# Attention scores leave their PSUM bank at the row maximum, and the exponential runs in place in SBUF

## The chip, the cores and the metric

One core of one Trainium2 chip runs the whole program in one launch. The metric is device time in microseconds (us). A core has TensorE (PE), VectorE (DVE), ScalarE (ACT) and GpSimd (POOL), a queue that issues the DMAs (SP), SBUF (128 partitions), and eight PSUM banks of 128 x 512 fp32 values.

## What is computed

A decoder layer over x of shape (4, 512, 512) fp32: self-attention with 16 heads of 32 columns, a mixing step with the weights of a context, and a feed-forward part of 4096 columns with packed 4-bit weights. The change touches the self-attention alone. Masked scores there are multiplied by zero, not set to minus infinity:

```python
scores = jnp.einsum('bthd,bshd->bhts', q, k)
mask = jnp.tril(jnp.ones((T, T), dtype=scores.dtype))
scores = scores * mask
attn = jax.nn.softmax(scores / T ** 0.5, axis=-1)
out = jnp.einsum('bhts,bshd->bthd', attn, v).reshape(B, T, H * Dh)
return out @ Wo
```

## The kernel before

The order on each engine is written out by hand; engines meet through semaphores. There are four batches n. The attention of a batch is a body of 16 units u (`UNITS`) between two stretches of other work (`between`: projections, the context, the mixing). Unit u takes the four heads of head group `u // 4` and the 128 query rows of tile `i = u % 4`; only the `wide[i]` = 128 (i + 1) keys at or below the diagonal are handled, the others through one exponential of the negated maximum (`exp_zero`, `masked_values`). In this text (u, j) is head j of unit u, and four units of one head group are called a group: units 8 to 11 are one.

For each (u, j) the steps are:

- `scores` (PE, L929): one matmul into `bank[j]`. Bank j is used by head j of every unit, so the matmul of (u + 1, j) waits until (u, j) has left it. Before, that is `exp_done` of (u, j).
- `row_max` (DVE, L1600): multiplies the scores by mask and factor and takes the row maximum. It writes the product back into `bank[j]`, and a second short instruction writes the maximum into `mx`.
- `shift` (POOL, L763): negates the maximum into `nmx`.
- `exp` (ACT, L1257): reads `bank[j]`, adds `nmx`, writes `prob[:, u % 2, j]` in SBUF; a second short instruction on the same line reads the sum into `den`.
- `turn` (PE, L940): transposes `prob` in blocks of 128 x 128 into bank 4, 5 or 7, which three turns, reciprocals and packed weights share in rotation; a turn waits for the reader of the one three places before it (`turn_read`).
- `turned` (ACT L1273, for three heads, or two in the last unit of a group; DVE L1610 for the others): copies the bank into `prob_t`.
- `values` (PE, L961): probabilities times values of a whole unit into bank 6; `recips` (PE, L970) and `recip_out` (ACT, L1279) lay out the reciprocals, `divide` (DVE, L1638) makes `o_sum`; `out_head` (ACT, L1285) and POOL's `out_tail` (L779) split a finished group.

PE's order sets much of the rest. In unit u it is

```python
for j in range(4):
    if u + 1 < UNITS:
        scores(n, u + 1, j)
    turn(n, u, j)
    ...
    if j == 3 and u > 0:
        recips(n, u - 1)
        if u < UNITS - 1:
            values(n, u - 1)
```

POOL converts packed weights (L756) beside it, PE and ACT repack them at j = 1 and j = 3 of the first unit of a group (`repack`, ACT's copy `pk_t` L1293). DVE's order in unit u is `row_max(u, 0)`, `divide`, `row_max(u, 1)`, then `all_tokens(u - 1)`, which waits for all four exponentials of unit u - 1, `row_max(u, 2)`, `row_max(u, 3)`, and a copy.

`prob` has other tenants between the bodies: the context's exponentials (`e_p`, half 1), the first block of weights and the operands of sums (half 0), which DMAs store from it.

Of the kernel before, what the change touches and what calls it, by code (L numbers as in the profile page):

```python
# [47 lines left out]
B, T, D = 4, 512, 512  # L48
# [43 lines left out]
def decoder_layer(nc, x, ctx_1024, Wq, Wk, Wv, Wo, xWq, xbq, xWk, xbk, gate_p, gate_s, up_p, up_s, down_p, down_s, out):  # L92
    with ExitStack() as ctx:
# [236 lines left out]
        def alone(eng, sem, value):  # L330

            eng.wait_ge(sem, value)
            eng.sem_inc(passed, 1)
# [539 lines left out]
        def _(pe):  # L873
# [43 lines left out]
            def scores(n, u, j):  # L917
                hg, i = u // TT, u % TT
                if i == 0 and j == 0:
                    for g in (2 * hg, 2 * hg + 1):  # L920
                        pe.wait_ge(stacked[g % 4], n * 128 + 64 * (g // 4) + 64)
                if u > 0:
                    pe.wait_ge(exp_done, n * ROWS + 4 * (u - 1) + j + 1)
                elif j == 2:
                    pe.wait_ge(v_out, n * TT + 3)
                elif j == 3:
                    pe.wait_ge(vb_out, n * (TT - 1) + TT - 1)
                h = 4 * hg + j
                pe.matmul(bank[j][:, 0:wide[i]], stack[:, 0, h, P * i:P * i + P], stack[:, 1, h, 0:wide[i]],  # L929
                          start=True, stop=True).then_inc(s_full, 1)  # L930
# [299 lines left out]
        def _(act):  # L1230
# [21 lines left out]
            def exp(n, u, j):  # L1252
                i = u % TT
                act.wait_ge(shift_done, n * ROWS + 4 * u + j + 1)
                if u >= 2:
                    act.wait_ge(t_full, n * ROWS + 4 * (u - 2) + j + 1)
                nc.scalar.activation(prob[:, u % 2, j, 0:wide[i]], bank[j][:, 0:wide[i]], ACT.Exp,  # L1257
                                     bias=nmx[:, u % 2, j:j + 1], accum_out=den[:, u % 2, j:j + 1]).then_inc(exp_done, 1)

            def exp_zero(n, u):  # L1260
# [131 lines left out]
            def between(n, prev, nxt):  # L1392
# [49 lines left out]
                    spread_heads(2, n, 4)  # L1442
                if nxt:
                    context_heads(n + 1, (0, 1))
                    if n == B - 2:
                        act.wait_ge(sums_stored, 16 * 8)
                    elif n >= 0:
                        act.wait_ge(first_stored, 16 * (3, 7)[n])
                    exp(n + 1, 0, 0)
                    exp(n + 1, 0, 1)  # L1450
                    context_heads(n + 1, (2, 3))
                    exp(n + 1, 0, 2)
                    exp(n + 1, 0, 3)
                    qkv_heads(n + 1, (11,))
# [28 lines left out]
            def body(n, last):  # L1483
                for u in range(UNITS):
                    for j in range(4):
                        if u == 1 and j == 0:
                            act.wait_ge(att_full, n * KT + KT)
                        if u > 0:
                            exp(n, u, j)
                        if j == 3 and u % TT < TT - 1:  # L1490
                            exp_zero(n, u)
                        if j == AT_OUT and u % TT == 2 and u > TT:
                            out_head(n, u // TT - 1)

                        if j >= 2:
                            turned(n, u, j - 2)
                        elif j == 0 and u > 0:
                            if copied_by_act(u - 1) > 2:
                                turned(n, u - 1, 2)
                        if j == 3 and u % TT == 0 and u > 0:  # L1500
                            repacked(n, u // TT - 1)
                        h = 4 * u + j - AT_RECIP
                        if h >= 0 and h % 4 == 0:
                            recip_out(n, h // 4)
                turned(n, UNITS - 1, 2)
                if not last:
                    spread_heads(0, n + 1, 0)
                for u in range((ROWS - 1 - AT_RECIP) // 4 + 1, UNITS - 1):
                    recip_out(n, u)
                repacked(n, HG - 1)  # L1510
                recip_out(n, UNITS - 1)
                out_head(n, HG - 1)
                between(n, True, not last)
# [28 lines left out]
        def _(dve):  # L1542
# [51 lines left out]
            def row_max(n, u, j):  # L1594
                i = u % TT
                if u >= 2:
                    dve.wait_ge(shift_done, n * ROWS + 4 * (u - 2) + j + 1)
                alone(dve, s_full, n * ROWS + 4 * u + j + 1)

                nc.vector.tensor_tensor_reduce(out=bank[j][:, 0:wide[i]], in0=bank[j][:, 0:wide[i]],  # L1600
                                               in1=mask[:, P * (3 - i):P * (3 - i) + wide[i]], scale=C_EXP,
                                               scalar=0.0 if i < TT - 1 else NEG, op0=ALU.mult, op1=ALU.max,
                                               accum_out=mx[:, u % 2, j:j + 1]).then_inc(max_done, 1)
# [215 lines left out]
            def between(n, prev, nxt):  # L1819
# [32 lines left out]
                    spread_tails(2, n, 4)  # L1852
                if nxt:
                    value_sum_out(n + 1, 2)
                    row_max(n + 1, 0, 0)
                    row_max(n + 1, 0, 1)
                    context_tails(n + 1, (0, 1))
# [177 lines left out]
```

## Time and profile before

| | us |
|---|---|
| median of 3 runs | 1482.5 (1481.33 to 1483.2) |
| profiled execution | 1482.48 |
| its span, first to last instruction | 1480.8 |
| PE busy in the span | 1426.6 (96%) |
| DVE busy | 990.7 (67%) |
| ACT busy | 716.4 (48%) |
| POOL busy | 380.2 (26%) |

The shares are means over very different stretches. The attention bodies lie at about 66 to 128, 196 to 260, 328 to 392 and 465 to 530 us of the span; behind the last comes the feed-forward part, with PE busy throughout. Times in the rows below are microseconds from the span's start.

### The profile page before, as it was taken

The page shows a single profiled execution, that of the slowest core. Times are in us where ns is not written, and L with a number is a line of the kernel's source. Part 1 is how long each engine was busy: PE and PEld are TensorE (multiplying, and loading weights), DVE is VectorE, ACT ScalarE, POOL GpSimd, SP SyncE. Part 2 cuts the span into 40 slices and gives each one's busy share as a digit, 9 for nine tenths or more (in the row PEclk, how much of TensorE's full clock was granted, in tenths as well). Part 3 has the DMA queues.
Part 4 walks back from the last instruction along what each step waited for, and adds up shares of the span by engine and source line. Part 5 has one row for each costly group of instructions (what it writes and reads, how often), then busy time and mean ns, then how long its engine had stood idle before and what let it go on. Part 6 is the DMA issues. An engine that isn't in the chain of part 4 may idle for free.

```text
span 1480.8 us, 26838 instructions
## 1 busy us (share of the span) xinstructions
PE 1426.6 (96%) x8896; PEld 720.5 (49%) x8896; DVE 990.7 (67%) x2125; ACT 716.4 (48%) x1660; POOL 380.2 (26%) x691
## 2 busy tenths in 40 slices
PE   6989998998998899999999999999999999999999
PEld 4465456556644654344444444444444444444444
DVE  7786688678668767887566666655765765665533
ACT  5795279239615945254353353353343442533432
POOL 0053225304363436512211112112112212212100
PEclk9999999999999999999999999999999999999999
DMA  7554522352454521000000001001001001000011
GB/s 249 136 166 125 155 86 81 111 163 66 147 154 137 195 81 45 17 16 33 22 13 32 17 17 33 17 17 35 17 17 32 17 16 33 17 17 1 0 58 57
DMA packets 76877, 98.01 MB, mean 66 GB/s; under 512 B 8000, under 2 KB 60736, under 8 KB 76224
## 3 DMA queue, kind: packets, MB, share of 16 engines
q1 hardware_dynamic: 76736, 96.23, 21.2%
q8 instruction: 76, 1.25, 0.4%
q14 instruction: 65, 0.53, 0.1%
HBM read 68.94 MB, written 27.26 MB: 65 GB/s over the span
## 4 chain that ended last, share of the span: by engine, by line
PE 83%; DVE 5%; issue 5%; ACT 4%; POOL 1%; DMA 1%; ACTq 0%; POOLq 0%; SPq 0%; DVEq 0%
PE bank L876 24%; PE bank L877 24%; PE bank L878 24%; PE bank L940 2%; ACT prob L1257 2%; PE bank L961 2%; PE bank L1016 1%; PE bank L929 1%; PE bank L889 1%; PE bank L970 1%; PE bank L1011 1%; PE bank L1001 1%; DVE xt L1585 1%; DMA pk_in<-L_ffn_down_W_packed_dram 1%; ACT prob_t L1273 1%
## 5 line engine op out<-in xcount | busy, mean ns | idle before, releaser
L876 PE MATMUL bank<-xs,G 128*128 128x512 f16 x896 | 339.8, 379 | 2.0 <-DVE c L1730 0.9
L878 PE MATMUL bank<-xs,G 128*128 128x512 f16 x896 | 339.6, 379 | 0.0
L877 PE MATMUL bank<-xs,G 128*128 128x512 f16 x896 | 339.6, 379 | 0.0
L1345 ACT COPY c<-bank 128x512 f32<-128x512 f32 x192 | 111.2, 579 | 220.0 <-PE bank L878 215.2
L1730 DVE TENSOR_TENSOR c<-bank,c 128x512 f32<-128x512 f32 x128 | 88.1, 689 | 193.0 <-PE bank L878 193.0
L876 PE MATMUL bank<-Wd,hid 128*128 128x512 f16 x512 | 194.1, 379 | 2.8 <-DVE X L1784 2.8
L878 PE MATMUL bank<-Wd,hid 128*128 128x512 f16 x512 | 194.0, 379 | 0.0
L877 PE MATMUL bank<-Wd,hid 128*128 128x512 f16 x512 | 194.0, 379 | 0.0
L748 POOL TENSOR_TENSOR c<-c,m 128x512 f32<-128x512 f32 x64 | 82.4, 1287 | 388.5 <-ACT c L1345 388.5
L1784 DVE SCALAR_TENSOR_TENSOR X<-bank,col,X 128x512 f32<-128x512 f32 x128 | 95.4, 750 | 101.5 <-PE bank L878 101.4
L1600 DVE CUSTOM_DVE_ANT_0 bank<-bank,mask,col 128x128 f32<-128x128 f32 (+3 forms) x256 | 139.1, 548 | 23.0 <-issue 17.8
L1257 ACT ACTIVATE prob<-bank,nmx 128x128 f32<-128x128 f32 (+3 forms) x256 | 145.7, 577 | 1.5 <-POOL nmx L763 0.9
L876 PEld LDWEIGHTS bank<-xs,G 128*128 128x128 f16 x896 | 87.6, 98 | 113.3 <-ACT c L1345 6.1
L878 PEld LDWEIGHTS bank<-xs,G 128*128 128x128 f16 x896 | 87.7, 98 | 105.8
L877 PEld LDWEIGHTS bank<-xs,G 128*128 128x128 f16 x896 | 87.7, 98 | 103.1
L940 PE MATMUL bank<-ident,prob 128*128 128x128 f32 x640 | 111.9, 277 | 13.3 <-ACT prob L1257 4.5
L1368 ACT CAST hid<-c 128x512 f16<-128x512 f32 x128 | 79.2, 619 | 90.3 <-DVE c L1744 87.2
L1360 ACT ACTIVATE c<-c,col 128x512 f32<-128x512 f32 x96 | 69.4, 723 | 94.1 <-DVE c L1730 94.1
L763 POOL TENSOR_TENSOR nmx<-zero,mx 128x1 f32<-128x1 f32 x256 | 51.1, 199 | 238.8 <-DVE mx L1600 215.5
L1750 DVE TENSOR_TENSOR hid<-c,hid 128x512 f16<-128x512 f32 x128 | 86.1, 712 | 25.7 <-ACT hid L1368 25.7
L705 POOL TENSOR_TENSOR w_sum<-w_full 128x384 f32<-128x384 f32 (+1 forms) x30 | 22.1, 738 | 314.2 <-DVE w_full L1711 314.1
L940 PEld LDWEIGHTS bank<-ident,prob 128*128 128x128 f32 x640 | 76.1, 140 | 31.3 <-issue 18.9
(192 smaller groups left out, 2409.1 us busy)
## 6 DMA issues: line engine op xcount, KB each, us to landing
stack<-qk_dram SPq DMA_DIRECT2D x128, 128.0 KB, 3.3
sc_in<-scale_t SPq DMA_DIRECT2D x30, 384.0 KB
qk_dram<-qk SPq DMA_DIRECT2D x32, 256.0 KB, 2.9
packed_t<-pk_t SPq DMA_DIRECT2D x32, 192.0 KB, 1.9
pk_in<-packed_t SPq DMA_DIRECT2D x30, 192.0 KB
X<-in_x_dram SPq DMA_DIRECT2D x4, 1024.0 KB, 5.7
pk_in<-L_ffn_gate_W_packed_dram SPq DMA_DIRECT2D x16, 256.0 KB, 2.7
pk_in<-n_L_ffn_up_W_packed_dram SPq DMA_DIRECT2D x16, 256.0 KB, 3.0
```

The costliest lines, as they stand in the source:

```text
L748: nc.gpsimd.tensor_tensor(c22[x][:], c22[x][:], m5[x][:], ALU.add).then_inc(c22_out, 1)
L876: pe.matmul(o, lhs(0), rhs(0), start=first, stop=False, skip_group_check=onto)
L877: pe.matmul(o, lhs(0), rhs(1), start=False, stop=False, skip_group_check=onto)
L878: return pe.matmul(o, lhs(1), rhs(0), start=False, stop=stop, skip_group_check=onto)
L940: mm = pe.transpose(turn_bank(slot)[:, P * k:P * k + P], prob[:, u % 2, j, P * k:P * k + P], ident[:])
L1257: nc.scalar.activation(prob[:, u % 2, j, 0:wide[i]], bank[j][:, 0:wide[i]], ACT.Exp, bias=nmx[:, u % 2, j:j + 1], accum_out=den[:, u % 2, ...
L1345: nc.scalar.copy(dst[:], bank[BANK_Y if which == M5 else x][:]).then_inc(c_copied, 1)
L1368: nc.scalar.copy(hid[:, beta, q, r, 0, :], quarter(1, idx)[:]).then_inc(hid_hi, 1)
L1600: nc.vector.tensor_tensor_reduce(out=bank[j][:, 0:wide[i]], in0=bank[j][:, 0:wide[i]], in1=mask[:, P * (3 - i):P * (3 - i) + wide[i]], sca ...
L1730: nc.vector.tensor_tensor(dst[:], bank[at][:], dst[:], ALU.add).then_inc(comb, 1)
L1750: nc.vector.tensor_tensor(hid[:, beta, q, r, 1, :], quarter(1, idx)[:], hid[:, beta, q, r, 0, :], ALU.subtract).then_inc(hid_lo, 1)
L1784: nc.vector.scalar_tensor_tensor(xv, bank[4 + t][:], C_OUT, xv, ALU.mult, ALU.add).then_inc(acc_out, 1)
```

## The change

The product of `row_max` goes to `prob` in SBUF instead of back into the bank. The exponential reads it there and writes over it. A bank is free as soon as the maximum is taken, so `scores` of (u + 1, j) waits for `max_done` of (u, j). The waits that protect `prob` move with its first writer, from ACT to DVE: the turn of two units before (`t_full`), the context's transposes (`att_full`), and the stores of what lay in half 0 (`first_stored`, `sums_stored`).

```diff
--- before.py
+++ after.py
@@ scores (PE)
                 if u > 0:
-                    pe.wait_ge(exp_done, n * ROWS + 4 * (u - 1) + j + 1)
+                    pe.wait_ge(max_done, n * ROWS + 4 * (u - 1) + j + 1)
@@ exp (ACT)
                 act.wait_ge(shift_done, n * ROWS + 4 * u + j + 1)
-                if u >= 2:
-                    act.wait_ge(t_full, n * ROWS + 4 * (u - 2) + j + 1)
-                nc.scalar.activation(prob[:, u % 2, j, 0:wide[i]], bank[j][:, 0:wide[i]], ACT.Exp,
+                nc.scalar.activation(prob[:, u % 2, j, 0:wide[i]], prob[:, u % 2, j, 0:wide[i]], ACT.Exp,
@@ between (ACT)
                     context_heads(n + 1, (0, 1))
-                    if n == B - 2:
-                        act.wait_ge(sums_stored, 16 * 8)
-                    elif n >= 0:
-                        act.wait_ge(first_stored, 16 * (3, 7)[n])
                     exp(n + 1, 0, 0)
@@ body (ACT)
-                        if u == 1 and j == 0:
-                            act.wait_ge(att_full, n * KT + KT)
@@ row_max (DVE)
                 if u >= 2:
                     dve.wait_ge(shift_done, n * ROWS + 4 * (u - 2) + j + 1)
+                    dve.wait_ge(t_full, n * ROWS + 4 * (u - 2) + j + 1)
+                elif u == 1 and j == 0:
+                    dve.wait_ge(att_full, n * KT + KT)
                 alone(dve, s_full, n * ROWS + 4 * u + j + 1)
 
-                nc.vector.tensor_tensor_reduce(out=bank[j][:, 0:wide[i]], in0=bank[j][:, 0:wide[i]],
+                nc.vector.tensor_tensor_reduce(out=prob[:, u % 2, j, 0:wide[i]], in0=bank[j][:, 0:wide[i]],
@@ between (DVE)
                     value_sum_out(n + 1, 2)
+                    if n == B - 2:
+                        dve.wait_ge(sums_stored, 16 * 8)
+                    elif n >= 0:
+                        dve.wait_ge(first_stored, 16 * (3, 7)[n])
                     row_max(n + 1, 0, 0)
```

No instruction is added, taken away or moved to another place on its engine. What differs is what they wait for and where they read and write. On PE, in unit 2 of a batch with the scores of unit 3 (L929) between the turns (L940), before:

```order
L929 MATMUL bank<-stack 128x512 [waits exp_done]
L940 MATMUL bank<-ident,prob 128x128 [waits rden_out,exp_done]
L940 MATMUL bank<-ident,prob 128x128 x2
L929 MATMUL bank<-stack 128x512 [waits exp_done]
L940 MATMUL bank<-ident,prob 128x128 [waits pt_act,exp_done]
```

and now:

```order
L929 MATMUL bank<-stack 128x512 [waits max_done]
L940 MATMUL bank<-ident,prob 128x128 [waits rden_out,exp_done]
L940 MATMUL bank<-ident,prob 128x128 x2
L929 MATMUL bank<-stack 128x512 [waits max_done]
L940 MATMUL bank<-ident,prob 128x128 [waits pt_act,exp_done]
```

The scores matmul keeps its place ahead of the turn, but no longer waits for the exponential that the turn behind it waits for. On DVE, the row maxima of unit 3 (128x512) with the small work between them, before:

```order
L1600 ISA bank,mx<-bank,mask,col 128x512 [waits shift_done,s_full]
L1600 ISA mx 128x1
L1618 SCALAR_TENSOR_TENSOR den_all<-e_zero,den 128x4 [waits e_zero_done,exp_done]
L1600 ISA bank,mx<-bank,mask,col 128x512 [waits shift_done,s_full]
L1600 ISA mx 128x1
L1628 RECIPROCAL r_col<-den_all 128x4 [waits den_done]
```

and now (the lines after the edits are five lower):

```order
L1595 ISA prob,mx<-bank,mask,col 128x512 [waits s_full,shift_done,t_full]
L1595 ISA mx 128x1
L1613 SCALAR_TENSOR_TENSOR den_all<-e_zero,den 128x4 [waits e_zero_done,exp_done]
L1595 ISA prob,mx<-bank,mask,col 128x512 [waits s_full,shift_done,t_full]
L1595 ISA mx 128x1
L1623 RECIPROCAL r_col<-den_all 128x4 [waits den_done]
```

The row maximum has one wait more and writes to `prob`; the instruction between, which waits for the exponentials of the unit before, stands where it stood.

## Rows read from the trace of the kernel before

**Rows 1.** Windows: busy us and instruction count of PE, PEld, DVE, ACT, POOL; clock; DMA.

```profile
202.00:215.50 13.50, 11.79 (x155) 8.23 (x154) 12.08 (x47) 12.81 (x48) 6.27 (x25) 1.00 0.19 59
230.70:245.80 15.10, 13.58 (x205) 9.87 (x205) 12.54 (x50) 14.16 (x52) 7.31 (x26) 1.00 0.24 75
```

**Rows 2.** Scores matmuls, line 929: PE idle before them, by what ended it: us, times.

```profile
  ACT prob L1257: 43.7, 136
```

**Rows 3.** Timeline of ACT, units 8 to 11 of batch 1: start, duration, instruction, idle before.

```profile
231.03 0.27 ACT L1273 COPY prob_t<-bank 128x128 f32<-128x128 f32 x1 [0.54 <-PE bank L940]
...
234.80 0.37 ACT L1273 COPY prob_t<-bank 128x256 f32<-128x256 f32 x1 [0.38 <-PE bank L940]
...
242.50 0.60 ACT L1273 COPY prob_t<-bank 128x512 f32<-128x512 f32 x1
242.97 0.72 ACT L1257 ACTIVATE prob<-bank,nmx 128x512 f32<-128x512 f32 x1
243.55 0.23 ACT L1257 ACTIVATION_READ_ACCUMULATOR prob<-bank,nmx 128x1 f32 x1
```

**Rows 4.** Timeline of PE, same units: turn (8, 3), then around turn (11, 3).

```profile
232.75 0.30 PE L940 MATMUL bank<-ident,prob 128*128 128x128 f32 x1 [0.29 <-ACT pk_t L1293]
...
243.83 0.23 PE L929 MATMUL bank<-stack 128*128 128x128 f16 x1
243.93 0.63 PE L940 MATMUL bank<-ident,prob 128*128 128x128 f32 x4
...
245.84 0.27 PE L940 MATMUL bank<-ident,prob 128*128 128x128 f32 x1
```

**Rows 5.** Groups by form, ACT: the same function on SBUF and on PSUM.

```profile
L1360 ACT ACTIVATE c<-c,col 128x512 f32<-128x512 f32 x96 | 69.4, 723 | 94.1 <-DVE c L1730 94.1
...
L1360 ACT ACTIVATE c<-bank,col 128x512 f32<-128x512 f32 x32 | 22.0, 688 | 4.5 <-PE bank L878 4.0
```

**Rows 6.** Timeline of ACT, unit 14: a copy out of SBUF and its successor.

```profile
251.56 0.63 ACT L1285 CAST o_t<-o_sum 128x512 f16<-128x512 f32 x1
252.07 0.40 ACT L1273 COPY prob_t<-bank 128x256 f32<-128x256 f32 x1
```

**Rows 7.** Timeline of ACT, exponential (3, 3) of batch 1, end of the first stretch.

```profile
212.60 0.85 ACT L1257 ACTIVATE prob<-bank,nmx 128x512 f32<-128x512 f32 x1
```

**Rows 8.** Timeline, exponentials (11, 0) and (11, 1) of batch 1, and POOL's shift.

```profile
239.51 0.54 ACT L1273 COPY prob_t<-bank 128x384 f32<-128x384 f32 x1
239.87 0.77 ACT L1257 ACTIVATE prob<-bank,nmx 128x512 f32<-128x512 f32 x1
...
240.55 0.56 ACT L1273 COPY prob_t<-bank 128x384 f32<-128x384 f32 x1
240.98 0.71 ACT L1257 ACTIVATE prob<-bank,nmx 128x512 f32<-128x512 f32 x1
```

```profile
240.76 0.19 POOL L763 TENSOR_TENSOR nmx<-zero,mx 128x1 f32<-128x1 f32 x1 [1.07 <-DVE mx L1600]
```

**Rows 9.** Groups by form, DVE: output to PSUM and output to SBUF.

```profile
L1784 DVE SCALAR_TENSOR_TENSOR X<-bank,col,X 128x512 f32<-128x512 f32 x128 | 95.4, 750 | 101.5 <-PE bank L878 101.4
...
L1600 DVE CUSTOM_DVE_ANT_0 bank<-bank,mask,col 128x512 f32<-128x512 f32 x64 | 47.7, 748 | 0.2
```

**Rows 10.** Timeline, unit 15, batch 1: DVE's `divide`, exponential (15, 1), turn (15, 1).

```profile
254.63 0.29 DVE L1638 SCALAR_TENSOR_TENSOR o_sum<-bank,r_den 128x128 f32<-128x128 f32 x1 [0.81 <-issue]
```

```profile
256.02 0.79 ACT L1257 ACTIVATE prob<-bank,nmx 128x512 f32<-128x512 f32 x1
```

```profile
257.72 0.63 PE L940 MATMUL bank<-ident,prob 128*128 128x128 f32 x4 [0.64 <-DVE prob_t L1610]
```

**Rows 11.** Timeline of ACT, exponential (6, 2) of batch 3.

```profile
492.30 0.58 ACT L1257 ACTIVATE prob<-bank,nmx 128x384 f32<-128x384 f32 x1 [0.65 <-POOL nmx L763]
```

**Rows 12.** Stores of sums out of `prob`, and the first row maximum of batch 3.

```profile
L495 SPq DMA_DIRECT2D xt_dram<-prob x2: 637/743/849, 458.1 to 458.8; - x2
...
DMA to landing us min/median/max: 3.5/3.6/4.0
```

```profile
466.61 0.35 DVE L1600 CUSTOM_DVE_ANT_0 bank<-bank,mask,col 128x128 f32<-128x128 f32 x1
```

## The prediction

> **What bounds the kernel now.** I began with where PE waits, since the change takes a wait from PE. The source view of the scores matmul shows PE idle before it for 43.7 us in 136 cases, ended by the exponential [rows 2]. That is the sum at which the change aims. It says nothing yet of the end: behind each of these matmuls PE's next instruction is the turn of (u, j), and it waits for the same exponential. So I asked which engine fills a stretch. The windows over a group of batch 1, units 8 to 11, show ACT busy 14.16 of 15.10 us, PE 13.58, DVE 12.54; over units 1 to 3 ACT is busy 12.81 of 13.50 [rows 1]. The clock column is 1.00, the higher of the clock's two levels. ACT is the bound inside the attention bodies, and PE comes second.
>
> ACT's timeline then shows where it is not the bound. In a group it waits twice, both times for a turn: 0.54 us before its first copy of unit 8, 0.38 before that of unit 9 [rows 3]. Between them the path runs as follows. First wait: exponential (7, 3), turn (7, 3), reciprocals and values on PE without a gap, turn (8, 0), ACT's copy. Second wait: from that copy through exponential (8, 3) and the copy `pk_t` to turn (8, 3), which PE starts at 232.75 when `pk_t` is out [rows 4], again reciprocals and values, turn (9, 0), copy at 234.80. From there to the end of exponential (11, 3), started at 242.97, ACT runs with no wait of note, and turn (11, 3) begins the next round at 243.93 [rows 3, 4]. This chain is closed: the same steps come back 15.1 us later. Exponentials on it: nine in the long ACT run, (9, 3) to (11, 3), and one, (x, 3), in the short one. The other six of a group lie ahead of ACT's two waits and have room there.
>
> **The change part by part.**
>
> *The scores matmul no longer waits for the exponential.* It goes ahead while PE waits for the exponential anyway, and the turn behind it starts sooner by the matmul's own issue. At turn (11, 3) the two starts are 243.83 and 243.93, so 0.10 us [rows 4]. The last turn of a group is the one place of the chain where PE waits for an exponential; turn (8, 3) waits for `pk_t`, the turns (8, 0) and (9, 0) come behind PE's own work. So three times 0.10 in a batch, behind units 3, 7 and 11. The rest of the 43.7 us turns into waits of the turns or lies inside ACT's run. Nor do the maxima run far ahead: the first scores of a unit stand behind the values of an earlier one on PE, and DVE stands still before the third maximum of a unit for the four exponentials of the unit before.
>
> *The exponential reads SBUF.* No row of before shows this exponential on SBUF. The nearest is the gelu, fp32 and in place, with a column operand: 723 ns on SBUF, 688 from PSUM, so 35 ns more [rows 5]. ACT overlaps neighbours, so starts count more than durations: a 512-wide copy out of SBUF holds its successor back 0.51 us (251.56 to 252.07) [rows 6], one out of PSUM 0.47 (242.50 to 242.97) [rows 3], 0.04 more. Bounds are 0.035 and 0.046 (the two-digit rounding of those starts), and 0 if the in-place exponential should hide it; I take 0.04.
>
> The Trainium skill gives another figure (VectorE: DVE Perf Modes, "The TRN2 errata — SBUF-src ops pay a fixed extra latency per instruction"): ScalarE takes 224 cycles plus one an element from SBUF and 172 from PSUM, which at 1.2 GHz is an estimate of 0.043 us an instruction. With it the sum below would be +2.5 us instead of +2.2. It is the rule that speaks most against this change, and the rows above lie close to it.
>
> Cost on the chain of batches 0 to 2:
> - Units 1 to 3: the start of exponential (3, 3) stands behind eleven others of this run, 11 x 0.04 = 0.44. Its own row is 0.85 us against 0.72 at (11, 3) [rows 7, 3]: in a full run its end lags its start by 0.13 more. An issue that comes 0.04 later each time should use up such a lag; I take it as gone, -0.13. With -0.10 for the scores: +0.21.
> - The short run behind it: one exponential, +0.04.
> - Units 5 to 7 and 9 to 11, each: eight exponentials ahead of the last, +0.32; the last lasts 0.72 now, as it would from SBUF. -0.10 for the scores. Exponential (11, 1) starts 0.43 us behind the copy before it, the same pair one head earlier 0.36; it is held by the shift, which ends at 240.95 [rows 8]. As ACT gets later this 0.07 goes. +0.15, and +0.04 for the short run behind: +0.19.
> - Units 12 to 15: behind `pk_t` the batch's end hangs on POOL, not on exponentials. DVE's `divide` waits 0.81 us there for POOL's split of the group before, and turn (15, 1) waits for DVE's copy behind the maxima of unit 15 [rows 10]. Nothing is added while ACT stays within that: exponential (15, 1) ends at 256.81, 0.9 us ahead of the turn [rows 10], and some ten exponentials since `pk_t` cost 0.4.
>
> Sum: 0.21 + 0.04 + 2 x 0.19 = 0.63 us a batch, 1.9 over three. In batch 3 exponential (6, 2) waits 0.65 us for POOL [rows 11], which stands for packed weights from DRAM; that absorbs the delay of the exponentials ahead of it. Left are two of the eight in units 5 to 7 (0.08 - 0.10), 0.19 for units 9 to 11 without its short run's 0.04, and three short runs, 0.12: some 0.25, and I count 0.3. **Together +2.2 us.**
>
> *The maximum writes to SBUF.* Two DVE rows with a PSUM source and a column operand: output to PSUM 748 ns, output to SBUF 750 [rows 9]. So 0, within 5 ns either way; five maxima of a batch lie on the POOL path, 0.1 us over all. The Trainium skill (Advanced Engine Details and Errata, "The Read-Write Bubble") says that VectorE is closer to SBUF and should be used so. If that held for an output as its cycle table has it for a source, an estimate of 0.065 us (62 cycles at 0.96 GHz), the sum would be +0.9; the two rows show none of it, and they decide.
>
> *Moved waits.* The turn of two units before is long done when the maximum of (u, j) comes, since its scores matmul stands behind the turns of unit u - 2 on PE; 0. The context's transposes stand ahead of `scores(1, 0)` on PE; 0. The stores out of `prob` are tightest in batch 3: last issue at 458.8, landing at most 4.0 later, 462.8, against the first maximum at 466.61 [rows 12]. 3.8 us of cover; were it gone, everything behind on DVE, starting with the context's tails, would come later by what is missing. ACT has one wait fewer on each exponential; I take 0.
>
> The sum is made against the profiled execution, 1482.48 us (span 1480.8 and 1.7 around it), which is the median of the runs, 1482.5, to 0.02. So 1482.5 + 2.2 = **1484.7 us**.
>
> **The rivals.**
>
> *Dearer exponentials, slower than before.* The place is ACT's two long runs, the price 0.046 instead of 0.04 and the lag of exponential (3, 3) kept. The last exponential of a run then lasts longer too: units 1 to 3 cost 12 x 0.046 - 0.10 = 0.45, each of the two groups 9 x 0.046 - 0.17 = 0.24, and three short runs 0.14: 1.07 a batch, 3.2 over three and 0.4 in batch 3, +3.6: 1486.1. With the lag kept it decides from 0.039 an exponential (33 of them less 0.44 a batch, three times, and 0.4, against 3.0). For it: the starts of the copies. Against: the gelu's 35 ns, and that (11, 3), as much the end of a run as (3, 3), lasts 0.72 and has hardly a lag.
>
> *The bank's release does bring time, faster.* If ACT's two waits shrank by more than the issue of one matmul, since all maxima come sooner and PE's work in front of turn (x, 0) with them, up to 0.54 + 0.38 us a group would be had. Half of that, 0.46, over 16 groups is 7.4; less the 2.2 above, -5.2: 1477.3. It decides from 0.33 us a group, (3.0 + 2.2) / 16. For it: the 43.7 us [rows 2]. Against it: PE is busy without a gap ahead of both turns, on work that waits for exponentials or `pk_t`, not for scores.
>
> *The reading costs nothing, no change.* If the in-place exponential hides its longer read, the gains stay: 0.44 us a batch, -1.6 in all: 1480.9.
>
> *The change does not do what it says* (scores still come when they came, because PE is held at the turns): this holds for most of them already, and with the read's price is the forecast plus 1.2, 1485.9; it ends on the border and is in the first rival's chance.
>
> **How the numbers follow.** What a measurement of this kernel can tell from no change is 0.2%, 3.0 us. The forecast, +1 to +3, has 0.45; the dear exponential with the change that does nothing 0.30; no price for the read 0.08; faster by the bank 0.17. Within 0.2% are the forecast, the third rival and a little of the first: 0.54. Slower is 0.29, faster 0.17. The forecast's own range is 1483.4 to 1485.4. The range runs from 1480.0, which leaves most of the faster rival out, to 1487.0, above the first rival by 0.9 us for a dearer short exponential.
>
> **What the profile after would show.** Exponentials of 512 that last 0.71 now, with no lag [rows 8], last up to 0.03 more. Starts of exponential and accumulator read 0.58 us apart now (242.97, 243.55) [rows 3], 0.61 to 0.63 then. PE idle before line 929 for the exponential gone, and idle before line 940 grown by nearly as much. The group's period 15.1 us grown by 0.2, ACT's share of it still over 93%. Row maxima unchanged at 748 ns for 512 [rows 9]. The forecast is wrong if the period falls, if exponentials keep their spacing, or if DVE idles before the first maximum of a batch.

## The result, and the profile after

The changed kernel took 1485.87 us (median of 20 runs, 1482.7 to 1487.86), the kernel before, run beside it, 1482.72 (20 runs, 1479.86 to 1485.02): 3.15 us more, ratio 1.002, 95% interval 1.0013 to 1.0026. So it is slower, by about as much as this measurement can tell. The forecast was 1484.7 with a range of 1480.0 to 1487.0. The time lies in the range, 1.2 us above the point. It lies outside the forecast's own 1483.4 to 1485.4, and next to what two rivals had: the dearer exponentials at 1486.1 and the change that does not do what it says at 1485.9. The experiments have to say which it was.

The page of the profiled execution, with the busy times and the chain that ended last:

```profile
span 1484.5 us, 26835 instructions
...
PE 1426.2 (96%) x8896; PEld 714.2 (48%) x8896; DVE 989.7 (67%) x2125; ACT 721.3 (49%) x1660; POOL 380.5 (26%) x691
...
PE 82%; ACT 9%; DVE 5%; issue 3%; DMA 0%; POOL 0%; ACTq 0%; DVEq 0%; SPq 0%
```

ACT is busy for 4.9 us more (716.4 before) over 256 exponentials, and PE for as long as before. The windows of [rows 1] again: the first lies at the same times, though the body now starts 0.55 us later, the second is moved by 0.4 us and 0.2 us longer:

```profile
202.00:215.50 13.50, 11.76 (x133) 7.46 (x134) 11.78 (x48) 12.68 (x47) 6.35 (x25) 1.00 0.13 39
231.10:246.40 15.30, 13.57 (x211) 9.62 (x204) 12.45 (x51) 14.40 (x53) 7.24 (x27) 1.00 0.25 79
```

ACT fills 14.40 of 15.30 us, 94% as before. Its busy time grew by 0.24 us, the period of a group by as much (0.30 us over a window of the whole new period, 231.78 to 247.14). Where PE waits, from the source views of the scores matmul (L929) and of the turn (L940), in us and times. First the scores, then the turns, both in the changed kernel, and last the turns in the kernel before:

```profile
  issue: 10.4, 49
  DVE mx L1595: 2.2, 11
```

```profile
  ACT prob L1255: 55.1, 123
  issue: 19.6, 45
```

```profile
  ACT prob L1257: 13.1, 21
```

The 43.7 us of [rows 2] are gone from the scores. The turns wait 55.1 us for the exponential where they waited 13.1, so 42.0 us more. That is nearly the whole fate of the bank that is free sooner: the wait moved one instruction down on the same engine. Around turn (11, 3), the rows that answer to [rows 3, 4]; ACT first, then PE:

```profile
243.16 0.75 ACT L1255 ACTIVATE prob<-prob,nmx 128x512 f32<-128x512 f32 x1
...
243.88 0.60 ACT L1271 COPY prob_t<-bank 128x512 f32<-128x512 f32 x1
244.34 0.76 ACT L1255 ACTIVATE prob<-prob,nmx 128x512 f32<-128x512 f32 x1
244.97 0.22 ACT L1255 ACTIVATION_READ_ACCUMULATOR prob<-prob,nmx 128x1 f32 x1
```

```profile
244.96 0.22 PE L929 MATMUL bank<-stack 128*128 128x128 f16 x1
245.25 0.33 PE L940 MATMUL bank<-ident,prob 128*128 128x128 f32 x1
```

Exponential and accumulator read lie 0.63 us apart (0.58 before); the scores start 0.29 us ahead of the turn, no longer right in front of it; and the turn comes 0.15 us behind the end of the exponential (0.24 before). The forms of the exponential and of the row maximum, with busy time and mean ns of one:

```profile
L1255 ACT ACTIVATE prob<-prob,nmx 128x512 f32<-128x512 f32 x64 | 48.0, 751 | 0.0
...
L1255 ACT ACTIVATE prob<-prob,nmx 128x256 f32<-128x256 f32 x64 | 32.9, 514 | 0.7 <-POOL nmx L763 0.6
```

```profile
L1595 DVE CUSTOM_DVE_ANT_0 prob<-bank,mask,col 128x512 f32<-128x512 f32 x64 | 47.3, 739 | 1.1 <-PE bank L929 0.4 <-POOL nmx L763 0.2
...
L1595 DVE DVE_READ_ACCUMULATOR2_ANT mx<- 128x1 f32 x256 | 21.2, 83 | 0.0
```

The last row holds something that the forecast did not count: the short read of the maximum behind each row maximum took 141 ns before (36.1 us in 256) and takes 83 now.

**A yardstick finer than the runs.** Single runs of one kernel differ by 5 us (1479.86 to 1485.02 before). The traces show part of it. The values in front of turn (4, 0) of batch 3 wait for nothing that the profile shows, in the changed kernel

```profile
487.52 0.73 PE L961 MATMUL bank<-prob_t,V 128*32 128x128 f32 x17 [0.99 <-issue]
```

and from turn (3, 3) to turn (4, 0) of batch 3 it took 1.91 to 1.95 us in eight traces and 3.0 to 3.8 in six, and versions with and without the change are in both groups. The stretch between batches 2 and 3 took 77.6 or 79.3 us, likewise (79.3 both before and after). Neither follows the change. The bodies of batches 0 and 2 have no such places: in each trace their slips agree within 0.02 us. So below, beside the times, stand the starts of four turns in batch 2, from PE's timeline, as differences from the turn before (from turn (0, 0) to (3, 3), on to (7, 3), (11, 3) and (15, 3)), and the whole body. "Slip" is a body's length less that of the kernel before, and the last stretch, from (11, 3) to (15, 3), is called the tail.

| version | to (3,3) | (7,3) | (11,3) | (15,3) | body | slip |
|---|---|---|---|---|---|---|
| before | 11.40 | 15.12 | 15.11 | 15.62 | 57.25 | |
| after | 11.68 | 15.36 | 15.36 | 15.80 | 58.20 | +0.95 |
| undo_bank | 11.79 | 15.45 | 15.44 | 15.80 | 58.48 | +1.23 |
| undo_bank_read | 11.40 | 15.18 | 15.18 | 15.74 | 57.50 | +0.25 |
| product_only | 11.27 | 15.12 | 15.12 | 15.56 | 57.07 | -0.18 |
| wait_alone | 11.41 | 15.29 | 15.29 | 15.81 | 57.80 | +0.55 |
| swap_wait | 11.42 | 15.13 | 15.14 | 15.63 | 57.32 | +0.07 |
| before_no_wait | 11.42 | 15.13 | 15.13 | 15.62 | 57.30 | +0.05 |
| before_no_waits2 | 11.39 | 15.12 | 15.12 | 15.60 | 57.23 | -0.02 |
| no_t_wait | 11.58 | 15.38 | 15.38 | 15.64 | 57.98 | +0.73 |
| no_waits | 11.57 | 15.37 | 15.37 | 15.62 | 57.93 | +0.68 |
| hybrid_no_waits | 11.35 | 15.09 | 15.10 | 15.64 | 57.18 | -0.07 |
| split_no_waits | 11.33 | 15.07 | 15.08 | 15.61 | 57.09 | -0.16 |

Batch 0 has the same +0.95 as batch 2. Batch 1 has +1.08: its tail grew by 0.31 us (15.84 to 16.15) instead of 0.18, and undo_bank has the same 16.15 there. With the first, third and fourth of these stretches of batch 3, free of that gap, which add 0.29, 0.29 and 0.20, it is 3.8 us by the trace and 3.15 by the runs (1.9 to 3.9 by the interval). The stretches between the bodies are as long as before within 0.03 us, and the first maximum of batch 3 follows DVE's work before it without a gap: the moved waits for the stores cost nothing.

### The profile page after: what moved, and what is told of

Same layout as the page of the kernel before. It is cut to its first block, busy times and chain, and to the rows that moved or that the text cites. A ratio compares the mean times of both kernels' runs of the same rounds, so it can differ in the third digit from the quotient of the medians.

```text
span 1484.5 us, 26835 instructions
## 1 busy us (share of the span) xinstructions
PE 1426.2 (96%) x8896; PEld 714.2 (48%) x8896; DVE 989.7 (67%) x2125; ACT 721.3 (49%) x1660; POOL 380.5 (26%) x691
## 4 chain that ended last, share of the span: by engine, by line
PE 82%; ACT 9%; DVE 5%; issue 3%; DMA 0%; POOL 0%; ACTq 0%; DVEq 0%; SPq 0%
PE bank L876 24%; PE bank L878 24%; PE bank L877 24%; ACT prob L1255 5%; PE bank L961 2%; PE bank L940 2%; ACT prob_t L1271 2%; PE bank L1016 1%; PE bank L889 1%; PE bank L1011 1%; PE bank L1001 1%; PE bank L970 1%; PE bank L929 1%; DVE xt L1577 1%; ACT pk_t L1291 1%
## 5 line engine op out<-in xcount | busy, mean ns | idle before, releaser
L1595 DVE CUSTOM_DVE_ANT_0 prob<-bank,mask,col 128x128 f32<-128x128 f32 (+3 forms) x256 | 137.1, 540 | 30.0 <-PE bank L929 16.9
L1255 ACT ACTIVATE prob<-prob,nmx 128x128 f32<-128x128 f32 (+3 forms) x256 | 147.0, 577 | 0.7 <-POOL nmx L763 0.6
L940 PE MATMUL bank<-ident,prob 128*128 128x128 f32 x640 | 115.1, 283 | 26.8 <-ACT prob L1255 8.6
L940 PEld LDWEIGHTS bank<-ident,prob 128*128 128x128 f32 x640 | 72.4, 141 | 69.7 <-ACT prob L1255 46.5
```

The lines of the kernel that those rows point to most:

```text
L940: mm = pe.transpose(turn_bank(slot)[:, P * k:P * k + P], prob[:, u % 2, j, P * k:P * k + P], ident[:])
L1255: nc.scalar.activation(prob[:, u % 2, j, 0:wide[i]], prob[:, u % 2, j, 0:wide[i]], ACT.Exp, bias=nmx[:, u % 2, j:j + 1], accum_out=den[:, ...
L1595: nc.vector.tensor_tensor_reduce(out=prob[:, u % 2, j, 0:wide[i]], in0=bank[j][:, 0:wide[i]], in1=mask[:, P * (3 - i):P * (3 - i) + wide[i ...
```

## The experiments

The edits are against the changed kernel or the kernel before, as each says.

**Undo the bank's release** (undo_bank), against the changed kernel:

```diff
-                    pe.wait_ge(max_done, n * ROWS + 4 * (u - 1) + j + 1)
+                    pe.wait_ge(exp_done, n * ROWS + 4 * (u - 1) + j + 1)
```

> The changed kernel with one part undone: the scores matmul waits for the exponential again instead of for the maximum. My theory gives the release of the bank 0.07 to 0.10 us behind units 3, 7 and 11 of each batch and nothing anywhere else: 12 places, so 0.9 to 1.2 us more than the changed kernel (1485.9), some 1487.0, and 1.003 of the kernel before. Rival one, the release is worth nothing at all because the turns hold PE anyway: same time as the changed kernel. Rival two, the release is worth much more and the exponentials cost more than 0.04 us, the two being hidden in the sum: 3 us and more above the changed kernel, over 1489. In the trace PE's idle time before line 929, ended by the exponential, should come back to about 44 us, and that before line 940 fall by as much.

1486.35 us (7 runs), 1.0029 of before (1.0018 to 1.004). The runs alone don't part it from the changed kernel; the table does: +0.28 us in the body, 0.11, 0.09 and 0.08 of it behind units 3, 7 and 11, nothing in the tail. Batches 0 and 1 give the same, 0.26 and 0.27. The release works, at the three places forecast and nowhere else. That rules out the change that does nothing, and rival two's 3 us. Before line 929 the idle time is back:

```profile
  ACT prob L1255: 49.3, 150
  issue: 10.2, 48
```

**Undo the read as well** (undo_bank_read), against the kernel above. It leaves the softmax out: the exponential reads the raw scores and multiplies them by zero.

```diff
-                nc.scalar.activation(prob[:, u % 2, j, 0:wide[i]], prob[:, u % 2, j, 0:wide[i]], ACT.Exp,
-                                     bias=nmx[:, u % 2, j:j + 1], accum_out=...
+                nc.scalar.activation(prob[:, u % 2, j, 0:wide[i]], bank[j][:, 0:wide[i]], ACT.Exp,
+                                     bias=nmx[:, u % 2, j:j + 1], scale=0.0, accum_out=...
```

> As the run before it, and the exponential reads the bank in PSUM again, while the maximum still writes its product to SBUF. The exponential so reads the raw scores times a scale of zero instead of the masked ones: the softmax is not computed, the instruction has its old operands and sizes. Against the run before only the place of the exponential's source differs. Theory: 0.043 us for an exponential in ACT's long runs, 11 ahead of turn (3, 3), 8 in each of the two groups behind, one in each short run, less 0.10 for the lag of exponential (3, 3) and up to 0.07 for the shift: about 1.1 us a batch, three times, and less in batch 3, so 3 to 4 us under the run before it, 1483.2 to 1484.0. What stays over the kernel before is then the added wait of the maxima. Rival: the read costs nothing in time and the loss comes from the moved waits or from the product written to SBUF: 1 us or less below the run before it. Starts of exponentials behind one another in a full run should be 0.43 us apart from the copy ahead again, and 0.04 less than in the run before.

1483.43 us (12 runs), 1.0006 of before (0.9997 to 1.0014). The body is 0.98 us shorter: 0.39, 0.27, 0.26 and 0.06 by stretch. That is the price of reading SBUF. Exponentials (11, 2) and (11, 3) of batch 2, out of PSUM here, and out of SBUF in undo_bank:

```profile
374.77 0.69 ACT L1255 ACTIVATE prob<-bank,nmx 128x512 f32<-128x512 f32 x1
...
375.44 0.57 ACT L1271 COPY prob_t<-bank 128x512 f32<-128x512 f32 x1
375.91 0.70 ACT L1255 ACTIVATE prob<-bank,nmx 128x512 f32<-128x512 f32 x1
```

```profile
377.94 0.76 ACT L1255 ACTIVATE prob<-prob,nmx 128x512 f32<-128x512 f32 x1
...
378.66 0.61 ACT L1271 COPY prob_t<-bank 128x512 f32<-128x512 f32 x1
379.13 0.76 ACT L1255 ACTIVATE prob<-prob,nmx 128x512 f32<-128x512 f32 x1
```

From the first to the second exponential it is 1.14 us out of PSUM and 1.19 out of SBUF. But +0.25 a body (0.44 in batch 1) is left over the kernel before, though scores and exponentials read and wait as they did there, apart from the waits that moved to DVE. By elimination it sits in the maxima.

**The added wait by itself** (wait_alone), against the kernel before:

```diff
                 if u >= 2:
                     dve.wait_ge(shift_done, n * ROWS + 4 * (u - 2) + j + 1)
+                    dve.wait_ge(t_full, n * ROWS + 4 * (u - 2) + j + 1)
```

> The kernel before with one line more and nothing else: from unit 2 on the row maximum also waits for the turn of two units before, which is always done by then. Theory from the two traces, where a maximum that stands waiting for its own scores starts 0.12 us later behind them in the changed kernel: an extra wait on DVE costs 0.12 us wherever DVE arrives early, which is at the first maxima of units 4, 8, 12 and in units 13 and 14, and the batch's tail behind unit 12 takes it up: 0.13 to 0.25 us a batch, so 0.5 to 1.0 us above the kernel before (1483.2 to 1483.7). Rival: a wait that is met costs nothing, the 0.12 us is the price of the product going to SBUF, or of something else: same time as the kernel before, and maxima that start as soon behind their scores as there.

1483.54 us (12 runs), 1.0007 (0.9999 to 1.0016), 1.1 us more by the medians, which is at the upper end of the theory. The body says more than that: +0.55 us (0.78 in batch 1), over twice the 0.13 to 0.25 expected. It is 0.17 and 0.18 to turns (7, 3) and (11, 3), where the theory had nothing, and 0.19 in the tail. A maximum for which DVE stood waiting starts later behind its scores: (14, 0) of batch 2, first with the wait, then in no_waits (below), without any extra wait:

```profile
382.48 0.34 PE L929 MATMUL bank<-stack 128*128 128x384 f16 x1
...
383.11 0.63 DVE L1601 CUSTOM_DVE_ANT_0 bank<-bank,mask,col 128x384 f32<-128x384 f32 x1 [0.82 <-PE bank L940]
```

```profile
382.96 0.34 PE L929 MATMUL bank<-stack 128*128 128x384 f16 x1
...
383.50 0.62 DVE L1590 CUSTOM_DVE_ANT_0 prob<-bank,mask,col 128x384 f32<-128x384 f32 x1 [0.75 <-PE bank L929]
```

0.63 us against 0.54; in the kernel before, with two waits, it is 0.52 (381.47 and 381.99). Note what the first row names as having ended the wait: the turn (L940), which had been done for a long time; it was put last in the instruction's waits. And in unit 11 the exponentials hang on the maxima. As in [rows 8], exponential (11, 1) starts 0.03 us behind the end of its shift, here 374.11; but it now comes 1.29 us behind exponential (11, 0) at 372.85, where it was 1.11.

```profile
373.92 0.19 POOL L763 TENSOR_TENSOR nmx<-zero,mx 128x1 f32<-128x1 f32 x1 [1.14 <-DVE mx L1601]
374.14 0.69 ACT L1257 ACTIVATE prob<-bank,nmx 128x512 f32<-128x512 f32 x1
```

**All extra waits of the maxima away** (no_waits), against the changed kernel; the scores matmul stands behind the turns and the context's transposes on PE, so the wait on it implies them:

```diff
-                if u >= 2:
-                    dve.wait_ge(shift_done, n * ROWS + 4 * (u - 2) + j + 1)
-                    dve.wait_ge(t_full, n * ROWS + 4 * (u - 2) + j + 1)
-                elif u == 1 and j == 0:
-                    dve.wait_ge(att_full, n * KT + KT)
```

> The changed kernel without the two or three waits in front of the row maximum besides that on its own scores (shift and turn of two units before, the context's transposes): the scores matmul itself stands behind all of them on PE, so it implies them. Theory: each wait less lets a maximum that arrives early start 0.12 us sooner: 0.13 to 0.25 us a batch for the wait that the change added and up to as much again for the older one: 0.5 to 1.7 us below the changed kernel, 1484.2 to 1485.4. Rival: waits that are met are free: the changed kernel's time. The row maximum of unit 5, 9, 13 and 14, head 0, should start 0.12 to 0.24 us sooner behind its scores matmul than in the changed kernel.

1483.3 us (12 runs), 1.0005 (0.9997 to 1.0014), body +0.68: 0.27 less than the changed kernel (0.42 in batch 1), 0.11 of it in units 1 to 3 and 0.18 in the tail, which is now as long as before. Four bodies of that are the 1.1 us in the middle of what was expected. The medians have 2.6, more than expected, and don't resolve the difference.

**The older wait away in the kernel before** (before_no_wait: the line on `shift_done` goes), **and the exponential's second wait too** (before_no_waits2: its two lines on `t_full` go):

> The kernel before without its own older extra wait: the row maximum no longer waits for the shift of two units before, only for its scores, which come later than that shift in any case. The run that added one such wait lost 0.55 us in a quiet batch (0.18 in each of units 7 and 11, where the last exponentials hang on the maxima, and 0.18 in the tail). Theory, that each wait costs DVE a fixed time whether it is met or not: the same again in the other direction, up to 0.5 us a batch less, but only as far as the maxima are still the last to come: 0.2 to 0.5 a batch, 1480.5 to 1481.6. Rival, only the second extra wait costs, the first is hidden in the one on the scores: 1482.4, and maxima that start no sooner behind their scores.

> As the run before it, and the exponential also drops its wait for the turn of two units before, so that it waits for the shift alone. The changed kernel had one wait fewer on ACT, and the forecast gave that 0. Theory: ACT fetches waits ahead of its pipeline and its exponentials keep their spacing: same time as the run before it, within 0.5 us. Rival: a wait on ACT costs as one on DVE does, 0.05 to 0.12 us an exponential in the full runs, of which some 30 a batch stand on the chain: 5 us less and more.

1481.75 us (11 runs), 0.9996 (0.9987 to 1.0005), and 1483.27 (11 runs), 1.0001 (0.9992 to 1.001); bodies +0.05 and -0.02. The theory that each wait has a price of its own, 0.2 to 0.5 us a body here, falls: with two waits and with one, DVE is equally fast. ACT's second wait in units 2 to 15 is worth 0.07 a body at most. What cost was the third on DVE. Two runs asked whether it is the count or the semaphore.

**The other wait in the older one's place** (swap_wait), against the kernel before, **and the changed kernel less its new wait** (no_t_wait: lines on `t_full` and `att_full` go, that on `shift_done` stays):

```diff
-                    dve.wait_ge(shift_done, n * ROWS + 4 * (u - 2) + j + 1)
+                    dve.wait_ge(t_full, n * ROWS + 4 * (u - 2) + j + 1)
```

> The kernel before with its older extra wait exchanged for the one that the change adds: the row maximum waits for its scores and for the turn of two units before, not for the shift of two units before. Two waits again, as before. So far: a third wait cost 0.55 us in a quiet batch, dropping the second brought nothing. Theory, the price hangs on the count (a third wait needs an instruction or a fetch of its own, the second is hidden): the slip of a quiet batch in the trace is 0 within 0.05. Rival, the price hangs on this semaphore, which PE raises: 0.5 a batch, as with both.

> The changed kernel with only the wait for the turn of two units before taken from the row maximum; the older one on the shift stays. By the count theory this is as good as taking both: in the trace 0.67 us a quiet batch over the kernel before, as without both, against 0.95 in the changed kernel. If each wait had its own price it would lie between, near 0.8.

swap_wait: 1482.77 us (10 runs), 1.0008 (0.9998 to 1.0017), body +0.07. no_t_wait: 1483.42 (10 runs), 1.0011 (1.0002 to 1.002), body +0.73, against 0.68 without any and 0.95 with all. Not the semaphore, then: the second wait is free or costs 0.05, the third 0.2 to 0.55. Maximum (14, 0) in swap_wait:

```profile
381.28 0.62 DVE L1600 CUSTOM_DVE_ANT_0 bank<-bank,mask,col 128x384 f32<-128x384 f32 x1 [0.70 <-issue]
```

Its scores started at 380.76, so 0.52 us; in the changed kernel it is 0.64 (383.93 and 384.57). Body +0.73 against 0.68 is 0.01 or 0.02 in each stretch, no more than the table resolves.

What the third wait does stands in the traces. The waits of a maximum are carried by semaphore instructions on DVE ahead of it. With one or two waits it is one instruction (on L333, in the helper `alone`). With three it is two, and the view below exists only in versions with a third wait; in the traces of before, swap_wait and no_t_wait nothing stands on L332. The row is of the changed kernel; 228 are 57 a batch, 56 maxima of units 2 to 15 and maximum (1, 0), which waits for a load besides:

```profile
L332 DVEq EVENT_SEMAPHORE  x228: 21/21/21, 70.2 to 529.2; - x114
```

So the change does add instructions, short ones that the program's text does not show. At maximum (14, 0) of wait_alone the one on L332 carries the wait on the scores and is through at 382.87, 0.39 us behind the start of the scores; the one on L333, with the two waits long met, runs from 382.92 to 382.97, and the maximum starts at 383.11. In swap_wait the only one, with both waits, is through at 381.15, also 0.39 us behind its scores, and the maximum starts at 381.28. The 0.10 us are the second semaphore instruction. The Trainium skill (Perfetto Trace Analysis, "Identifying Dependency Chains") says that further wait conditions of an instruction may stand in semaphore instructions of their own ahead of it, and these traces agree: it is the third wait here that needs one. So the count matters, and not which semaphore it is. What no run tells is whether the extra instruction would cost as much if the wait on the scores, which ends last, stood in the second one instead of the first. Per body the third wait costs 0.2 to 0.55 us, depending on what else is in the kernel.

**The product alone** (product_only), which is undo_bank_read less the maximum's lines on `t_full` and `att_full` (it leaves the softmax out too):

> Only one part of the change is left: the row maximum's product goes to SBUF. The exponential reads the raw scores in the bank, times a scale of zero (the softmax is not computed), the scores wait for the exponential, and the maximum has no more waits than before. Theory: the accumulator read behind the maximum is 0.06 us shorter (83 ns against 141), which made up for 0.3 of the 0.55 us a batch that the third wait cost, where the maxima were the last to come. Without that wait they are not: 0 to 0.05 us a batch less than before. Rival: it is a gain of its own, 0.3 us a batch less than before.

1480.76 us (10 runs), 0.9994 (0.9985 to 1.0003), body -0.18: between the two expectations. 0.13 comes at the start of unit 1, where exponential (1, 0) opens ACT's run: its shift ends 0.06 us earlier behind turn (0, 0) (1.10 us instead of 1.16), and it starts 0.03 us behind the shift instead of 0.09. The second half is not the product's: 0.03 stands in every trace in which ACT no longer waits for the context, undo_bank and undo_bank_read included, and 0.09 in every one in which it does. 0.06 more comes in the tail. In units 4 to 11 nothing. The accumulator read is short here as well, so it hangs on where the product goes, not on who reads it:

```profile
L1592 DVE DVE_READ_ACCUMULATOR2_ANT mx<- 128x1 f32 x256 | 21.7, 85 | 0.1
```

**A better version.** The release is worth having only where PE waits for an exponential, and the read costs only where ACT is the bound. hybrid_no_waits is before_no_waits2 with the change for head 3 of units 3, 7, 11 and 15 alone; split_no_waits, shown here, has it for units 12 to 15 too, where the path goes over POOL:

```diff
+        def in_sbuf(u, j):
+            return u >= UNITS - TT or (u % TT == TT - 1 and j == 3)
+
+        def scored(u, j):
+            return (prob[:, u % 2, j] if in_sbuf(u, j) else bank[j])[:, 0:wide[u % TT]]
...
-                    pe.wait_ge(exp_done, n * ROWS + 4 * (u - 1) + j + 1)
+                    released = max_done if in_sbuf(u - 1, j) else exp_done
+                    pe.wait_ge(released, n * ROWS + 4 * (u - 1) + j + 1)
```

with `scored(u, j)` as the maximum's output and the exponential's source.

> The run before it with the change made for one head in sixteen: only head 3 of units 3, 7, 11 and 15 has its product in SBUF and its bank free at the maximum, all other exponentials read PSUM. Theory: the release is worth 0.085 us at three places of a batch, the exponential there costs 0.043 less the lag that it uses up: 0.04 to 0.08 a place, 0.15 to 0.3 us a batch, so 0.6 to 1.2 us below the run before it, and the first of all versions clearly below the kernel before. Rival: the release is worth nothing without the other maxima being early as well: no gain, or 0.04 a place lost.

> As the run before it, and units 12 to 15 of each batch follow the change too: there the path goes over DVE and POOL, the exponentials have 0.9 us of room, and the maximum with its product in SBUF ends 0.06 us sooner by its accumulator read. Theory: the read's price lies in that room and the sooner maxima shorten the tail: in the changed kernel without the waits the tail was 0.3 to 0.4 us a batch shorter at turn (15, 3) than before; 0 to 0.2 us a batch below the run before it, so up to 0.8 us. Rival: the tail's exponentials cost more than their room: 0.1 to 0.3 us a batch above it.

> The fastest version so far a second time, to see whether it holds: its product in SBUF and its bank freed at the maximum only for head 3 of units 3, 7, 11 and for units 12 to 15, no wait in front of the maxima but that on the scores. By its slips, 0.17 us a quiet batch less than before, the time should be 0.7 us below the kernel before, ratio 0.9995; the 2.3 us of its first timing would then be mostly chance. If the ratio is 0.9985 again, something outside the batches' bodies gains as well.

hybrid_no_waits: 1481.53 us (11 runs), 0.9995 (0.9986 to 1.0004), body -0.07; each of the three places brings 0.02 to 0.04 against before_no_waits2, but the tail is 0.04 longer. That is 0.05 a body where 0.15 to 0.3 were expected, so the theory of this run missed. split_no_waits: 1480.23 (11 runs), 0.9990 (0.9981 to 0.9999), body -0.16, and a second time 1481.06 (11 runs), 0.9994 (0.9985 to 1.0003), body -0.17. Of the 0.09 by which its body is shorter than that of hybrid_no_waits only 0.03 lie in the tail. The rest lies in stretches in which the two programs are the same, 0.02 in each and in every batch, and no run here gives a cause. So a difference of 0.02 in a stretch of the table should not be read as an effect of the edit, which leaves little of what hybrid_no_waits brings. The ratios of the two timings together say 1.2 us under the kernel before, the bodies 0.7. By the bodies split_no_waits is the fastest of the versions that compute the softmax; the times can't show it, since the second interval includes no change.

## Why the prediction was right, and where it was not

In the order of its own steps; the numbers are for a quiet body (batch 2) unless another is named.

- **ACT is the bound, PE's 43.7 us are no gain**: right. The idle time went from line 929 to line 940, and of some 10.9 us of it in a batch the release brings 0.28.
- **The release, -0.10 at three places, -0.30**: measured -0.11, -0.09, -0.08, and 0 in the tail: -0.28.
- **The read, 0.04 an exponential**: net of the lag and of the shift's hold the sum had 0.31 for units 1 to 3, 0.29 for each of the two groups and 0.04 behind, 0.93. Measured 0.39, 0.27, 0.26, 0.06: 0.98. Within it, the lag of exponential (3, 3) gave 0.09 back and not 0.13 (0.85 before, 0.76 after, batch 1), and the spacing grew by 0.043 (from (1, 0) to (3, 3) of batch 1 it is 9.05 us before and 9.52 after, 0.47 over 11 exponentials). The gelu's 35 ns [rows 5] and the copies' 0.04 [rows 6] were the right neighbours. The Trainium skill's figure (VectorE: DVE Perf Modes, "The TRN2 errata — SBUF-src ops pay a fixed extra latency per instruction") gives an estimate of 0.043 us, and these traces agree with it.
- **Units 12 to 15, nothing**: false for the changed kernel, +0.18, and right without the waits: in no_waits the tail is as long as before, with all its exponentials out of SBUF. The room of 0.9 us held nearly: against product_only, whose tail is 15.56, it is 0.06 longer.
- **Moved waits, 0**: this is the step that failed. By itself the wait costs 0.55 us a body, with the product in SBUF 0.43 (undo_bank_read less product_only), and in the complete changed kernel 0.22 (after less no_t_wait), so the parts of the change overlap; that the slower exponentials hide some of the wait there is likely, and not shown. The argument, that it is always met, is true; what was not asked is what a met wait costs an instruction that has two others: a second semaphore instruction, 0.10 us. [rows 8] held the warning: exponential (11, 1) started 0.03 us behind its shift, so a maximum that comes later takes the exponential with it. The waits for the stores did cost nothing. The wait that ACT lost was taken as 0 as well, and gives 0.06 at exponential (1, 0).
- **The maximum's output, 0**: the instruction was 9 ns shorter (739 against 748), and the read behind it 58. That gives 0.12 back, 0.06 at unit 1 and 0.06 in the tail; with the 0.06 of ACT's wait it is product_only's 0.18. [rows 9] could not show it, since its row with an output in SBUF has no accumulator read behind it.
- **Batch 3, 0.3**: the trace has 0.78 in the three undisturbed stretches; the remaining one drowns in what differs from run to run. The forecast let ACT's wait of 0.65 us for POOL [rows 11] absorb the delay of the exponentials ahead of it. None of the other thirteen traces has that wait, so it was no term to build on.

The forecast per body, 0.63, was short of 0.95 by the wait, +0.43, by product and lost wait, -0.18, and by 0.07 in the others. This split holds for one order of undoing: with the wait taken at its 0.22 the read and the release are 0.28 above the forecast. By the trace the first three bodies have 2.98 us where the forecast had 1.9, and batch 3 0.78 instead of 0.3. That is 1.6 us above the point, where the runs have 1.2, which they don't tell from it.

So the mechanism of the forecast, the dearer read against a small gain from the release, is what happened, and that the time lay near enough is in part luck: two terms taken as 0 had opposite signs. The outcome just past 3.0 us is also not the one given the best chance, which was less than 3.0 (0.54, against 0.29 for slower). By place and sign the first rival was not what happened: the read cost 0.043 and the lag went for the most part; it landed on the time for another reason.

## What to carry to other kernels

A buffer that comes free sooner is worth what the next instruction on that engine gains, not the idle time in front of the first. Before paying for it everywhere, find the three places where it counts. When a change moves waits, count how many each instruction ends up with, and look for new semaphore instructions in the trace: a wait that is always met was not free here as the third on DVE, and often the wait on the producer implies it already.

## What the hardware showed that was not expected

- A row maximum (DVE) with two waits starts 0.52 us behind the start of its scores matmul of 384 columns, with one 0.54, with three 0.63 to 0.64, if DVE stands waiting for it. One or two waits make one semaphore instruction on DVE, three make two, and the second takes the 0.10 us.
- Exponential (1, 0), with a second wait on ACT that is long met, starts 0.09 us behind the end of its shift, without it 0.03, in all four batches of all traces.
- The accumulator read behind a DVE instruction takes 83 ns where that wrote its main output to SBUF, 141 where it wrote to PSUM (256 of each).
- The exponential of 512 columns lasted a mean of 774 ns out of PSUM before and 751 out of SBUF after, and the accumulator reads behind all exponentials 247 and 205, while the starts moved 0.04 us further apart. At 256 columns the exponential rose from 487 to 514. So durations fell where exponentials ran with a lag, and only the starts told the price.
